# One edge network with a mixture of experts: VectorE alone normalizes the node rows, small vectors are loaded as rows, and the first group's gathers move into the edge pass

## The reference

```python
def gnn(x, edge_index, edge_attr, ...):          # x is layernorm(x_in), E = 20000
    h = concat([x[dst], x[src], edge_attr], axis=1)
    gate = sigmoid(bn(silu(h @ W1f + b1f) @ W2f + b2f, g_int, beta_int))   # bn over all edges
    msg = gate * (silu(h @ W1m + b1m) @ W2m + b2m)
    agg = segment_sum(msg, dst, num_segments=625)
    return relu(x + bn(agg, g_bn, beta_bn))      # bn over all nodes
x = x_in + gnn(layernorm(x_in), ...)
# experts, on layernorm(x):
logits = xn @ Wg + bg + bias;  top 2, softmax over the two
h = relu(einsum('td,edh->teh', xn, W1) + b1)
y = einsum('teh,ehd->ted', h, W2) + b2
out = x + einsum('ted,te->td', y, combine)
```

## Time and profile before

| | |
|---|---|
| median of 3 runs | 829.78 us (829.55 to 830.56) |
| profiled execution, its own time | 830.01 us |
| its span in the trace | 828.0 us |
| granted TensorE clock, mean over the span | 0.971 |
| PE busy | 779.3 us (94%) |
| PEld busy | 674.4 us (81%) |
| DVE busy | 517.7 us (63%) |
| ACT busy | 451.6 us (55%) |
| POOL busy | 453.1 us (55%) |
| chain that ended last, from 684.55 us on | PE 15%, DVE 2% of the span |

### The profile page before, as it was taken

How to read it: one execution, slowest core, us unless ns; L and a number is a source line. 1 busy time by engine, 2 the same in 40 slices (tenths; PEclk the granted TensorE clock), 3 DMA queues, 4 the chain that set the end, 5 groups by cost and what they waited for, 6 DMA issues and landing times. The chain is left out here.

```text
span 828.0 us, 14465 instructions
## 1 busy us (share of the span) xinstructions
PE 779.3 (94%) x4534; PEld 674.4 (81%) x4535; DVE 517.7 (63%) x890; ACT 451.6 (55%) x794; POOL 453.1 (55%) x388
## 2 busy tenths in 40 slices
PE   4689999999999999999999989999999983999998
PEld 3467888888888888888888878888888872999998
DVE  3347665656566655556665457778788868555564
ACT  2434555554545555544455467776766672847570
POOL 1377777777777777777777145554545474000000
PEclk9889999999999999999999989999999995899999
DMA  6779999999999999999999867666555532003101
GB/s 178 208 253 344 340 354 325 326 344 324 342 335 332 341 335 327 326 333 340 335 333 333 300 235 243 213 238 216 205 205 218 204 110 101 1 28 101 51 25 32
DMA packets 68038, 201.47 MB, mean 243 GB/s; under 512 B 11446, under 2 KB 19162, under 8 KB 68010
## 3 DMA queue, kind: packets, MB, share of 16 engines
q1 hardware_dynamic: 41898, 118.12, 40.2%
q0 software_dynamic: 25024, 81.94, 29.9%
q10 hardware_dynamic: 1088, 1.05, 0.5%
HBM read 155.93 MB, written 45.14 MB: 243 GB/s over the span
## 5 line engine op out<-in xcount | busy, mean ns | idle before, releaser
L122 POOL DMA_INDIRECT pre<-table_dst,idx x157 | 171.8, 1095 | 49.4 <-issue 47.5
L434 POOL DMA_INDIRECT from_src<-table_src,idx x157 | 157.6, 1004 | 51.3 <-issue 47.2
L354 POOL TENSOR_TENSOR hvT_lo<-hv,hvT_hi 128x1024 fp32r<-128x1024 f32 x40 | 99.1, 2478 | 115.0 <-ACT hvT_hi L349 115.0
L565 PE MATMUL p_h<-eaT_hi,w_hi 128*128 128x512 f32 (+1 forms) x320 | 136.0, 425 | 1.5 <-DVE eaT_lo L490 1.5
L514 DVE TENSOR_TENSOR pre<-pre,from_src 128x512 f32<-128x512 f32 (+1 forms) x157 | 99.0, 691 | 44.3 <-DMA from_src<-table_src,idx 44.3
L565 PE MATMUL p_h<-eaT_hi,w_lo 128*128 128x512 f32 (+1 forms) x320 | 126.2, 394 | 0.0
L565 PE MATMUL p_h<-eaT_lo,w_hi 128*128 128x512 f32 (+1 forms) x320 | 125.7, 393 | 0.0
L528 DVE TENSOR_TENSOR h_lo<-h_full,h_hi 128x512 fp32r<-128x512 f32 (+1 forms) x80 | 54.4, 679 | 97.1 <-ACT h_full L469 96.8
L574 PEld LDWEIGHTS p_h<-ident,pre 128*128 128x128 f32 x628 | 77.5, 140 | 24.7 <-DVE pre L514 4.0
L574 PE MATMUL p_h<-ident,pre 128*128 128x128 f32 x628 | 94.1, 272 | 2.4 <-DVE pre L514 2.4
L468 ACT ACTIVATE h_hi<-p_h 128x512 fp32r<-128x512 f32 (+1 forms) x80 | 47.0, 587 | 89.7 <-PE p_h L574 89.7
(11 more groups left out here) (215 smaller groups left out, 1694.8 us busy)
## 6 DMA issues: line engine op xcount, KB each, us to landing
h_val<-hv_st SPq DMA_DIRECT2D x40, 512.0 KB, 4.6
z_gate<-zg_st SPq DMA_DIRECT2D x40, 512.0 KB, 7.7
hv<-h_val SPq DMA_DIRECT2D x40, 512.0 KB, 4.4
gate<-z_gate SPq DMA_DIRECT2D x40, 512.0 KB, 3.2
ea<-in_edge_attr_dram SPq DMA_DIRECT2D x39, 512.0 KB, 6.6
raw<-in_L_ffn_W_dram SPq DMA_DIRECT2D x16, 512.0 KB, 4.6
pre<-table_dst,idx POOLq DMA_INDIRECT x157, 6.3
from_src<-table_src,idx POOLq DMA_INDIRECT x157, 6.4
```

Of the source, the lines that this page charges most:

```text
L122: pool.indirect_dma_start(pre[b][0:n, t, :], None, table_dst, bass.IndirectOffsetOnAxis(ap=idx[b][0:n, t:t + 1], axis=0)).then_inc(got_dst ...
L354: nc.gpsimd.tensor_tensor(hvT_hl[b % 2][1][:], hv[b][:], hvT_hl[b % 2][0][:], ALU.subtract).then_inc(hv_lo, 1)
L434: pool.indirect_dma_start(from_src[b][0:n, t, :], None, table_src, bass.IndirectOffsetOnAxis(ap=idx[b][0:n, T + t:T + t + 1], axis=0)).the ...
L565: nc.tensor.matmul(p_h1[c][:, 0:w], w1_hl[wp][:, k, c * P:(c + 1) * P], eaT_hl[b % 2][dp][:, k, 0:w], start=n == 0, stop=False)
```

## The change

Three things change. First, the six small vectors are loaded as twelve rows of 512 bytes on ACT's queue at the program's start, transposed by PE beside the node numbers, and copied by ACT into `vecs`; SP's six loads at the end of the prologue are gone. Second, the load of group 1's edge features and the gathers of group 0's destination rows leave the prologue and stand at the head of the edge pass; each source gather of group 0 has a semaphore of its own, DVE sums its rows tile by tile as they land, and PE adds them tile by tile. Third, DVE does scale, shift, join and residual of all five tiles; POOL only makes its five additions, and begins them when all five tiles' low parts are there. PE no longer spreads scale and shift a second time, and it transposes tiles 3 and 4 after the first four pieces of the first product.

```diff
@@ -172,14 +172,11 @@
                         for lo, up in ROWS:
                             sp.dma_start(table_dst[t * TP + lo:t * TP + up, :],
                                          rows[0][lo:up, t, :]).then_inc(dst_stored, 16)
-                    load_ea(sp, 1, 1)
                     for t in range(NT):
                         sp.wait_ge(src_ok, t + 1)
                         for lo, up in ROWS:
                             sp.dma_start(table_src[t * TP + lo:t * TP + up, :],
                                          rows[1][lo:up, t, :]).then_inc(src_stored, 16)
-                    for n, v in enumerate((g_int, beta_int, b2f, b2m, g_bn, beta_bn)):
-                        sp.dma_start(vecs[:, n, :], column(v), allow_slow_non_contiguous=True).then_inc(v_in, 16)
...
                     pool.wait_ge(idx_ok, 4)
-                    gather_dst(pool, 0)
...
+                    for n, v in enumerate((g_int, beta_int, b2f, b2m, g_bn, beta_bn)):
+                        act.dma_start(vec_rows[n * KF:(n + 1) * KF, :], v.rearrange("(k p) -> k p", p=P)).then_inc(
+                            v_in, 16)
                     act.wait_ge(wab_in[0], 32)
                     nc.scalar.copy(w1ab_hl[0][:, 0], w1ab[:, 0]).then_inc(wab_hi, 1)
...
                     nc.scalar.copy(idx_num[:, 0:NF, :].rearrange("p g c -> p c g"), p_ids).then_inc(ids_spread, 1)
+                    nc.scalar.copy(vecs[:].rearrange("p n k -> p (n k)"), p_vec).then_inc(vec_ok, 1)
                     for t in range(NT):
...
-                    last.then_inc(ids_psum, 1)
+                    pe.wait_ge(v_in, 96)
+                    nc.tensor.transpose(p_vec, vec_rows[:], ident[0:6 * KF, 0:6 * KF]).then_inc(ids_psum, 1)
                     pe.wait_ge(wab_lo, 1)
...
 
+                    load_ea(sp, 1, 1)
                     for b in range(4):
                         step(0, b, first=True)
...
-                        if not (first and b == 0):
+                        if first and b == 0:
+                            gather_dst(pool, b)
+                        else:
...
-                                ap=idx[b][0:n, T + t:T + t + 1], axis=0)).then_inc(got_src[b], 16)
+                                ap=idx[b][0:n, T + t:T + t + 1], axis=0)).then_inc(
+                                    got_first[t] if first and b == 0 else got_src[b], 16)
 
...
-                    def sum_rows(i, b, short=False):
+                    def sum_rows(i, b, short=False, first=False):
                         rows = tiles(short)
                         dve.wait_ge(got_dst[b], 16 * T * i + 16 * len(rows))
-                        dve.wait_ge(got_src[b], 16 * T * i + 16 * len(rows))
+                        if not first:
+
+                            dve.wait_ge(got_src[b], 16 * T * (i - (b == 0)) + 16 * len(rows))
                         for t, n in rows:
+                            if first:
+                                dve.wait_ge(got_first[t], 16)
                             nc.vector.tensor_tensor(pre[b][0:n, t, :], pre[b][0:n, t, :], from_src[b][0:n, t, :],
                                                     ALU.add).then_inc(summed_ok, 1)
...
-                    sum_rows(0, 0)
+                    sum_rows(0, 0, first=True)
...
                             transpose_ea(1, 0, 1)
-                            for c in range(C):
-                                add_rows(g, b, c, False)
+                            for t in range(T):
+                                pe.wait_ge(summed_ok, t + 1)
+                                for c in range(C):
+                                    last = nc.tensor.matmul(p_h1[c][:, t * TE:(t + 1) * TE],
+                                                            pre[b][:, t, c * P:(c + 1) * P], ident[:],
+                                                            start=False, stop=t == T - 1, is_transpose=True)
+                                    if t == T - 1:
+                                        last.then_inc(h1_psum, 1)
                             second_layer(g, w, True)
                             return
...
-                    dve.wait_ge(v_in, 96)
+                    dve.wait_ge(vec_ok, 1)
...
-            p_scale, p_shift, p_st = p_h[3][0:TP, 0:F], p_b[0:TP, 0:F], p_a[0:TP, 0:2 * F]
+            p_scale, p_shift = p_h[3][0:TP, 0:F], p_b[0:TP, 0:F]
...
-                    pool.wait_ge(st_copied, 1)
-                    nc.gpsimd.tensor_tensor(xln[:, ND - 1, :], xln[:, ND - 1, :], st_rows[:, 1, :],
-                                            ALU.add).then_inc(pool_norm, 1)
-                    for t in range(ND, NT):
-                        n = 1 + 3 * (t - ND)
-                        nc.gpsimd.tensor_tensor(dev[:, t, :], agg[:, t, :], st_rows[:, 0, :],
-                                                ALU.mult).then_inc(pool_norm, 1)
-                        nc.gpsimd.tensor_tensor(xln[:, t, :], xln[:, t, :], st_rows[:, 1, :],
-                                                ALU.add).then_inc(pool_norm, 1)
-                        pool.wait_ge(pool_norm, n + 2)
-                        nc.gpsimd.tensor_tensor(dev[:, t, :], dev[:, t, :], xln[:, t, :],
-                                                ALU.add).then_inc(pool_norm, 1)
+                    pool.wait_ge(xnT_lo, NT)
                     for t in range(NT):
                         cols = slice(t * TP, (t + 1) * TP)
-                        pool.wait_ge(xnT_lo, t + 1)
                         nc.gpsimd.tensor_tensor(xnT[:, :, cols], xnT_hl[0][:, :, cols], xnT_hl[1][:, :, cols],
                                                 ALU.add).then_inc(xnT_ok, 1)
...
-                    act.wait_ge(st_psum, 3)
-                    nc.scalar.copy(st_rows[:].rearrange("p a f -> p (a f)"), p_st).then_inc(st_copied, 1)
...
+                    def scale(t):
+                        nc.vector.tensor_tensor(dev[:, t, :], agg[:, t, :], p_scale, ALU.mult).then_inc(scaled, 1)
+
+                    def shift(t):
+                        nc.vector.tensor_tensor(xln[:, t, :], xln[:, t, :], p_shift, ALU.add).then_inc(shifted, 1)
+
+                    def join(t):
+                        dve.wait_ge(scaled, t + 1)
+                        dve.wait_ge(shifted, t + 1)
+                        nc.vector.tensor_tensor(dev[:, t, :], dev[:, t, :], xln[:, t, :], ALU.add).then_inc(joined, 1)
+
+                    def residual(t):
+                        dve.wait_ge(joined, t + 1)
+                        nc.vector.scalar_tensor_tensor(out=x_sb[:, t, :], in0=dev[:, t, :], scalar=0.0,
+                                                       in1=x_sb[:, t, :], op0=ALU.max, op1=ALU.add).then_inc(x1_ok, 1)
+
                     dve.wait_ge(st_psum, 1)
                     for t in range(ND):
-                        nc.vector.tensor_tensor(dev[:, t, :], agg[:, t, :], p_scale, ALU.mult).then_inc(scaled, 1)
+                        scale(t)
                     dve.wait_ge(st_psum, 2)
-                    for t in range(ND - 1):
-                        nc.vector.tensor_tensor(xln[:, t, :], xln[:, t, :], p_shift,
-                                                ALU.add).then_inc(shifted, 1)
-                    for t in range(ND):
-                        dve.wait_ge(scaled, t + 1)
-                        if t < ND - 1:
-                            dve.wait_ge(shifted, t + 1)
-                        else:
-                            dve.wait_ge(pool_norm, 1)
-                        nc.vector.tensor_tensor(dev[:, t, :], dev[:, t, :], xln[:, t, :], ALU.add).then_inc(joined, 1)
-                    for t in range(ND):
-                        dve.wait_ge(joined, t + 1)
-                        normalize_sum(t)
+                    for stage in (shift, join, residual):
+                        for t in range(ND):
+                            stage(t)
                     ln_statistics(0, ND)
+                    for t in range(ND, NT):
+                        scale(t)
                     ln_apply(0, ND, 0)
-                    for t in range(ND, NT):
-                        dve.wait_ge(pool_norm, 1 + 3 * (t - ND + 1))
-                        normalize_sum(t)
                     ln_lo(0, ND)
+                    for stage in (shift, join, residual):
+                        for t in range(ND, NT):
+                            stage(t)
                     ln_statistics(ND, NT)
                     ln_apply(ND, NT, 1)
                     ln_lo(ND, NT)
...
                     pe.wait_ge(scale_ok, 1)
                     spread_column(p_scale, 2).then_inc(st_psum, 1)
-                    spread_column(p_st[:, 0:F], 2)
                     pe.wait_ge(shift_ok, 1)
                     spread_column(p_shift, 4).then_inc(st_psum, 1)
-                    spread_column(p_st[:, F:2 * F], 4).then_inc(st_psum, 1)
-                    for t in range(NT):
-                        pe.wait_ge(xn_ok, t + 1)
-                        for k in range(KF):
```

(14 more changed lines are left out.)

19 lines of the change are left out of this document (8 added, 11 removed).

## The result

The changed kernel is slower: 836.25 us, median of 20 runs (831.55 to 838.31), against 830.46 for the kernel before in the same sitting (20 runs); ratio 1.0056, 95% interval 1.0042 to 1.0070. The forecast was 828.4, within 826.9 to 831.0. The medians lie 5.79 us apart and the means 4.8, since the executions of the changed kernel spread over 6.8 us.

A forecast was written before the change was run, and what follows sets the result against it. PE runs nearly without a gap, so shifts at the edge pass's head, where gathers set the long run's start, and in the experts' stage carry through: +0.7 - 2.1 = -1.4 us, from 829.78 to 828.4, range 826.9 to 831.0.

The forecast's parts named there:

- Vector loads: Prologue: without SP's vector loads PE opens the edge pass at 34.3, 4.0 us sooner; ACT's row loads cost 0.
- Gathers moved: Head of edge pass: source gathers and group 1's rows 1.1 us later, partly absorbed to +0.7, bounds -0.1 and +1.5.
- The first rival: Edge pass: clock falls while PE waits for group 1, costing 2.0 us; time 829.9; chance 0.25.
- +0.7 of the rows: Edge pass: net delay taken from group 1's later rows after full DMA engines absorb part, bounds -0.1 and +1.5.
- the prediction's own signs of being wrong: Edge pass: source gathers before 39.3, clock falling around 60 us, or group 1's wait not the last that matters.
- The DMA rival: Edge pass: DMA engines are the bound, 1.5 MB entering it adds 4.1 us; time 831.8; chance 0.10.
- Normalization: Experts' stage: DVE normalizing alone brings the router's product 2.1 us sooner, bounds 1.1 and 2.8.
- The rival of strict turns: Experts' stage: DVE and POOL exclude each other during POOL's additions, gain only 1.1 us; time 829.4; chance 0.07.

The follow-up runs named there:

- The hold: Changed kernel, with SP's first store of hidden values waiting until group 1's rows have landed: 830.07 us, ratio 0.9998 to the kernel before.
- putting the gathers back: Changed kernel with group 0's four destination gathers issued ahead of the block's end again: 835.93 us, ratio 1.0059 to the kernel before.
- the sixteen matmuls: Changed kernel plus sixteen unread matmuls on PE while it waits for group 1's rows: 833.76 us, ratio 1.0042 to the kernel before.
- the edge half alone: Changed start and edge pass with the experts' stage of the kernel before: 836.50 us, ratio 1.0062 to the kernel before.
- fillings: Kernel before with new normalization, plus six unread matmuls behind the later nodes' transposes (829.11 us), or these and thirteen more at PE's wait for normalized nodes (828.70 us).
- the six matmuls: Kernel before with new normalization, plus six unread matmuls on PE behind the last transposes of the nodes: 829.11 us, ratio 0.9971 to the kernel before.

## Why the prediction was wrong

*Vector loads.* Right: ACT was not held up (7.89, had 7.96), and PE opened at 34.71, expected 34.3.

*Gathers moved: this is the step that failed.* Its issues were right in kind and somewhat small: the first source gather at 40.64 (forecast 40.0), 1.70 later than before where 1.5 was the bound, and group 1's last tile 1.75 us late (forecast 1.1). What failed is "group 1's rows come 1.1 us later too" and the bounds of -0.1 and +1.5 that rest on it. I priced the landing as unchanged and looked for other traffic only in total: 29% of the DMA engines' time free at 51 us. But SP's store of group 0's hidden values stayed at 54.95, and the tile slid from 1.78 to 0.14 us ahead of it; that cost 2.76 us more of landing, 4.5 in sum. The hold shows it: without the collision the tile lands in 3.9 us and the time is that of the kernel before. Moving group 0 forward and group 1 back meets the same collision from either side, which is why putting the gathers back did not help.

*The first rival was the other half.* It said that the clock falls while PE waits for group 1, and priced that at 2.0; it fell, and cost 13.82 - 11.08 = 2.7 by group 2, which the sixteen matmuls took back in their trace. I had it as the alternative to a +0.7 of the rows, not on top of +4.5. The Trainium skill's "TensorE: Matmul & The Clock Gate", section "HAM oscillation — how this bites in real kernels", which the prediction named for this rival, agrees with the rows here: a wait of 3.33 us, then a stretch at 0.50, and the same after 3.46 us with the hold. The rows in the experts' stage show a fall that no wait explains.

*Not foreseen: POOL's long issues.* With PE late, rows are there before VectorE asks for them, so in groups 2 to 4 it runs from the counting into the sums without a gap, and POOL's issue lasts until that run is over. Three of these in the changed kernel put the gathers behind them back, and PE waits again at group 7: +2.0 from group 6 to 7 in the table at the top. That these issues cost just that is argued from the table; that their end hangs on VectorE's run is shown, in one execution. So two of the prediction's own signs of being wrong came true: the clock fell at the wait for group 1, and that wait was not the last that mattered.

*The DMA rival* (slower, 831.8) had the right place and the wrong reason. While the tile was under way the engines were nearly full: share 0.95, 0.88 and 0.98 over 56 to 58, 58 to 60 and 60 to 62 us, after 0.64 over 54 to 56. But it was not the 1.5 MB more in the pass that made the tile late: the hold moves as many bytes in another order, and the tile lands in 3.9 us.

*Normalization.* -2.1 at the router's product was right (-2.22 in the changed kernel), and by the path forecast: the first piece came 8.17 us after the first shift, before 13.20. The rival of strict turns, which gave 1.1, is out: POOL's five additions took 0.89 each beside VectorE's subtractions, as forecast. That the gain is carried on was wrong: PE's first second product came 33.1 and 32.8 us after the scale's spreading with the old normalization (before, and the edge half alone), and with the new one 31.4 to 31.8 in five executions and 32.5 to 32.9 in seven. In the seven the clock fell to 0.50 in expert 1's first product; it did so in two of the five as well, but there the router's product had come a microsecond sooner (21.0 and 20.6 us after the spreading, in the others 21.75 to 22.35). So about 1.4 us or 0.3 are kept up to there.

A second fall of the clock, shortly before the end, parts the same traces once more. In the seven, and in both with the old normalization, the clock is at 0.50 for some 3.4 us between 815 and 829 us, and the program ends 106.2 us after the first second product. In the five it stays at 1.00 until about a microsecond before the end, which comes after 104.7. The rows of the kernel before and of the hold, with the columns of the earlier trace rows:

```profile
817.30:820.60 3.30, 3.30 (x18) 3.30 (x17) 0.99 (x3) 0.00 (x0) 0.00 (x0) 0.50 0.14 39
```

```profile
817.70:820.90 3.20, 3.20 (x29) 3.20 (x28) 1.28 (x3) 0.00 (x0) 0.00 (x0) 1.00 0.29 80
```

From the scale's spreading to the end this makes 139.1 and 139.3 us with the old normalization, 138.7 to 139.1 in the seven and 136.1 to 136.4 in the five. Against those two traces the new normalization is thus worth 0.6 us at most or about 3, by how the clock happens to fall. In the medians it is 0.4 us, and 1.8 and 2.2 with fillings whose effect beside it is not shown. Why the clock falls there in some executions stays open; that PE waits is ruled out for the first fall by the six matmuls, and around the second PE had no gap at all (busy for 103.20 of the 103.20 us from 717.3 on in the kernel before).

*Still open:* with the hold the edge pass begins its long run later than before the change: PE's adds of group 1 come 33.54 us after the first store of the source table, before 32.32, and the 1.2 us have grown to 2.4 at group 7. The first source gather is 1.4 us late by the same measure (12.86 against 11.42), which fits, but was not tried apart.

## What to carry to other kernels

When a step moves, price not only its own issue but who stands next to it on the DMA engines: list, for the transfer that the critical engine waits for, which bulk transfers are issued within two microseconds of it (here 1.8 us were enough and 1.05 were not), on every queue, before and after the move. An earlier start of one stage can be worth nothing, or less, if it lets that stage's stores overtake the next stage's rows; one wait on SP gave 5 to 6 us back. And a wait that grows on TensorE is to be priced with the half clock behind it from the start. Before a trace is read as the cause of a median, compare the time of its execution with that median: here they lay up to 6 us apart.

## What the runs showed of the hardware that was not expected

- A gather of 128 rows of 2 KB took 3.6 to 4.2 us to land when issued 1.76 us or more ahead of a 512 KB store and a 512 KB load (seven traces), 4.9 at 1.05 us, and 6.8 to 8.0 when issued 0.14 us ahead to 0.41 behind (five traces).
- POOL's issue of a gather, 0.95 us alone, lasted in thirteen cases until 0.82 to 0.86 us after the end of a run of VectorE that goes from its counting through the edge features and the adds without a gap: 3.09 to 3.86 us, and 4.58 with the run made longer. Beside 62 such runs without the counting, issues took at most 1.46 us. The Trainium skill's "SBUF — State Buffer", section "Who interferes with whom", lets VectorE and GpSimd shut each other out at a port that they share, but infers that `tensor_tensor` does not hold up the making of descriptors; the 62 agree with that, and the run made longer by three `tensor_tensor` adds, whose issue ended later by as much, speaks against it, as far as it is the adds that the issue waits for.
- The granted clock fell to 0.50 after 10 us in which TensorE was busy for 9.56, and stayed at 1.00 after 9.40 us in which it was busy for 7.51.
